# A macaron layer with two mixture-of-experts FFNs: where the first FFN's expert results are put, how empty rows are filled, who takes the roots

## The chip, the cores and the metric

One core of one Trainium2 chip runs the whole kernel in one launch. The metric is the device time in microseconds; a kernel is timed in several runs, and one more execution is profiled.

## The reference, cut to what matters

The input is x of 4 x 512 tokens with 256 features. Three residual steps follow each other, all in fp32:

```python
x = x + 0.5 * ffn(layernorm(x))      # FFN 0
x = x + attention(layernorm(x))      # 16 heads of 128, 4 sequences of 512
x = x + 0.5 * ffn(layernorm(x))      # FFN 1, the same weights
# ffn(t):
logits = t @ router_w.T              # 16 experts
w, e = top_k(softmax(logits), 2);  w = w / sum(w)
shared = silu(t @ sg) * (t @ su) @ sd                       # 256 hidden
routed = sum over k of w[k] * (silu(t @ gate[e[k]]) * (t @ up[e[k]])) @ down[e[k]]   # 128 hidden
return shared + routed
```

Each of the 2048 tokens goes to two experts, so an FFN has 4096 expert rows, and how many an expert gets is known only on the chip. Weights of attention come as codes and block scales that the kernel multiplies.

## The kernel before, in words

Matrix products are made of three products of a high and a low part (fp32r), `product`, lines 1324 to 1330. x lies in SBUF (`X`) as 16 tiles of 128 tokens; a quarter `q` or batch `b` is four of them (512 tokens).

**Routing.** For each quarter `statistics` (L857) takes mean and variance; `rstd` takes the root of 1/variance: ScalarE makes Ln and Exp (L608 to L615), VectorE one Newton step (L869). ScalarE and VectorE normalize into `rows`, TensorE transposes, `logits` (L1344) and `choose` pick the two experts, `ranks` and `positions` give each expert row its place in `xs_dram`, a DRAM array with a region of 2176 rows for each expert. GpSimd's `scatter` (L468) writes every tile of normalized rows twice, once for each choice, by indirect DMAs of 128 rows (L492); a row carries as word 257 the place of its result, which a small copy (L463, "marking") sets, so the second choice's marking waits for the first choice's landing.

**Empty rows.** Expert rows are worked through in 48 tiles of 128 rows, in 24 pairs; an expert's last tile has rows that nobody wrote. So VectorE's `free_rows` gives SP the row behind each expert's last one, and SP's `fills` (L321) copy 128 empty rows behind each expert, 16 DMAs (all before the first tile load in FFN 0, 12 in FFN 1). `tables_expert` and `tables` (L944, L956) make, on one partition, the list of tile offsets (`toff`) and of the tiles' experts (`words`), which SP and TensorE load into registers.

**Tiles.** `tiles` of PE, ACT and DVE (L1401, L647, L999) are one loop, shifted by stage: pair p+1 is transposed (L1418), pair p goes through gate and up, its silu and product follow, p-1 is transposed again (L1440), p-2 goes through down. ScalarE evicts a pair's result (L674) into one of two buffers `dnb`; GpSimd's `results` (L499) scatters each tile of it by an indirect DMA (L502) to `y_dram`, in the order of the tokens, at the places in word 257. The eviction waits until the buffer's scatters before have landed; SP's `tile_loads` (L332) wait for the landing too, as a tile's rows hold the places. In FFN 0 the expert weights' halves are split inside the loop, one chunk per pair (`split_hi`, `split_lo`, three staging buffers), 11 of 18 chunks before it (`PRE_CHUNKS`).

**Around the tiles.** The shared FFN runs in steps of 512 tokens: `EARLY` = 2 of its four steps before the tiles, the rest after (`shared_late`). When the results have landed, SP loads them for each batch (`y_loads`), VectorE adds them with their weights (`combine_half`), and the next normalization follows. GpSimd prepares attention's weight parts (`weights`, L522) that SP loads (`part`, L364; one codes DMA and four scales DMAs each); the first four parts are loaded behind the last tile load.

**Attention.** 64 units, one for a head and a batch. Tables written by hand name the unit in which an extra piece runs: `START` and `MID` (V blocks "V", transposes "Ta" and "T1"), `COMBINE`, `STATS` and `RSTD` (L277 to L292). In VectorE's order the insertion `before_scores` (L1178) stands ahead of the row maxima of the next unit; ScalarE's `exp_` waits for those. Between the units GpSimd also splits expert weights for FFN 1 and writes them to DRAM; SP loads them back near the end.

Of the kernel before, what the change touches and what calls it, by code (L numbers as in the profile page):

```python
# [5 lines left out]
P = 128  # L6
# [14 lines left out]
KT = D // P  # L21
# [6 lines left out]
LN_EPS = 1e-5  # L28
SM_SCALE = float(HD) ** -0.5
# [6 lines left out]
ROW = D + 1  # L36
NR = 48
# [9 lines left out]
PRE_CHUNKS = 11  # L47

EARLY = (2, 2)
FIRST_PRE = 3  # L50
SECOND_PRE = 9

FILLS_FIRST = (NE, 12)
# [4 lines left out]
C_ID, C_IOTA, C_J, C_EB, C_LT, C_I = 0, 128, 144, 160, 176, 432  # L58
C_POW = C_I + NR
C_N = C_POW + 6  # L60
# [47 lines left out]
class Views:  # L108
# [4 lines left out]
    "cst_in rw_in rw tri pads b_in bo_in bo bias w_hi w_lo e_in dv av pool_steps "  # L113
    "pre_in pre_mul pre_out "
# [11 lines left out]
def build(nc, t):  # L126
    with ExitStack() as ctx:
        def sb(name, shape, dt=F32):
# [15 lines left out]
        m.ln = sb("ln", [P, 2, 5, QB])  # L144
# [10 lines left out]
        m.tab = sb("tab", [1, 6, NE])  # L155
        m.frow = sb("frow", [1, NE], I32)
# [3 lines left out]
        m.mx = sb("mx", [P, QB])  # L160
        m.sm = sb("sm", [P, QB])
        m.ri = sb("ri", [P, QB])
        m.bank = [ctx.enter_context(nc.psum_tensor(f"bank{i}", [P, 512], F32)) for i in range(8)]
        m.xs_dram = [nc.dram_tensor(f"xs_dram{f}", (XROWS, ROW), F32, kind="Internal").ap() for f in range(2)]
# [22 lines left out]
        m.rows = Yw.rearrange("p (t d) -> p t d", t=NT)  # L187
        m.yb = Yw[:, 0:TOPK * QB * D].rearrange("p (b k t d) -> p b k t d", b=1, k=TOPK, t=QB)
        m.y1 = m.PT.rearrange("p l b n -> p (l b n)")[:, 0:TOPK * QB * D].bitcast(F32)\
            .rearrange("p (k t d) -> p k t d", k=TOPK, t=QB)  # L190
# [9 lines left out]
        m.ind = c.cut(NR // 2 * NE)[0:1].rearrange("p (t e) -> p t e", e=NE)  # L200
        m.te = c.cut(2 * NR)[0:1].rearrange("p (a t) -> p a t", a=2)
        m.rwT = c.cut(KT * NE).rearrange("p (k e) -> p k e", k=KT)
        m.sg = Pw[:, 4 * D:4 * D + 2 * S].rearrange("p (j n) -> p j n", j=2)
        m.dnb = Pw[:, 0:2 * 2 * D].rearrange("p (b n) -> p b n", b=2)
        m.sgr = Pw[:, 4 * D:4 * D + 4 * P].rearrange("p (b j n) -> p b j n", b=2, j=2)
# [39 lines left out]

        @block.tensor
        def _(pe):
            pe_program(nc, pe, m, s)


XS_F = 16 * (NR // NT)
RES_F = 16 * (NR // 4)


def chunk_place(m, c):

    if c < SH_CHUNKS:
# [1522 lines left out]
```

## Time and profile before

| | us |
|---|---|
| median of 3 runs (lowest, highest) | 1249.88 (1244.11, 1250.19) |
| the profiled execution's own time | 1238.46 |
| its span, first to last instruction | 1236.7 |
| TensorE busy | 1108.0 (90%) |
| VectorE busy | 856.8 (69%) |
| ScalarE busy | 719.2 (58%) |
| GpSimd busy | 372.7 (30%) |
| mean granted TensorE clock | 0.963 |

The span falls into routing and one half of the shared FFN (to 84 us), the first tile loop (to 174), a handover (to 212), attention (to about 1070), routing again (to 1115), the second tile loop (to about 1204) and an end. Busy shares are averages over these stages. The ends of matmuls are modelled, and a wait is put down to what came last by the profile.

### The profile page before, as it was taken

To read this page: it belongs to the slowest core of one execution; us is meant where nothing else is said; L and a number is where in the kernel's file an instruction comes from. 1 tells how busy PE (TensorE), PEld (TensorE's weight loads), DVE (VectorE), ACT (ScalarE), POOL (GpSimd) and SP (SyncE) were. 2 spreads that over 40 slices of the span, in tenths; PEclk is the share of its full clock that TensorE was granted. 3 is DMA by queue.
4 is the path that set the end of the run, shared out by engine and by line. 5 is a ranking of instruction groups with operands and counts; after the bars stand their busy time and mean duration, and the time that the engine had idled before them with its cause. 6 is when DMAs were issued, how large, how long until landed. Compare 5 with 4: busy or idle time off the path is not lost.

```text
span 1236.7 us, 20720 instructions
## 1 busy us (share of the span) xinstructions
PE 1108.0 (90%) x6360; PEld 957.0 (77%) x6360; DVE 856.8 (69%) x1837; ACT 719.2 (58%) x1485; POOL 372.7 (30%) x458
## 2 busy tenths in 40 slices
PE   5759984799999999999999999999999999858994
PEld 5648873687888878888888888888888877747884
DVE  7455436788777787877778777787777777653336
ACT  5226432666766766767767676676767666424441
POOL 2714567220003463400154320124001042342550
PEclk9869997899999999999999999999999999978997
DMA  4546435020013104400022430011000012655425
GB/s 172 186 151 185 139 102 165 10 69 1 1 54 118 41 24 153 129 5 1 18 65 87 144 95 1 9 35 53 1 1 1 2 62 105 236 171 144 135 81 204
DMA packets 58602, 103.76 MB, mean 84 GB/s; under 512 B 12756, under 2 KB 41819, under 8 KB 57952
## 3 DMA queue, kind: packets, MB, share of 16 engines
q1 hardware_dynamic: 50816, 85.60, 22.2%
q0 software_dynamic: 7680, 16.84, 3.8%
q8 instruction: 55, 0.90, 0.3%
q14 instruction: 51, 0.42, 0.1%
HBM read 70.89 MB, written 40.16 MB: 90 GB/s over the span
## 4 chain that ended last, share of the span: by engine, by line
PE 75%; DVE 7%; issue 6%; ACT 4%; DMA 3%; SPq 2%; another core or an unknown queue 2%; POOL 1%; POOLq 0%; DVEq 0%; ACTq 0%
PE bank L1327 14%; PE bank L1329 14%; PE bank L1328 14%; PE bank L1546 9%; PE bank L1554 5%; PE bank L1556 4%; PE bank L1555 4%; PE bank L1573 2%; PE bank L1572 2%; PE bank L1571 2%; PE bank L1418 1%; DMA y_dram<-work 1%; PE bank L1338 1%; POOL y_dram L502 1%
## 5 line engine op out<-in xcount | busy, mean ns | idle before, releaser
L1327 PE MATMUL bank<-R 128*128 128x512 f32 (+2 forms) x1056 | 405.0, 384 | 57.9 <-DVE X L996 21.3
L1328 PE MATMUL bank<-R 128*128 128x512 f32 (+2 forms) x1056 | 382.1, 362 | 0.0
L1329 PE MATMUL bank<-R 128*128 128x512 f32 (+2 forms) x1056 | 381.4, 361 | 0.0
L1327 PEld LDWEIGHTS bank<-R 128*128 128x128 f32 x1056 | 207.1, 196 | 99.0 <-issue 46.7
L1329 PEld LDWEIGHTS bank<-R 128*128 128x128 f32 x1056 | 206.7, 196 | 28.8
L1328 PEld LDWEIGHTS bank<-R 128*128 128x128 f32 x1056 | 207.7, 197 | 22.3
L1142 DVE TENSOR_REDUCE mx<-bank 128x1 f32<-128x512 f32 x256 | 174.5, 691 | 61.0 <-PE bank L1329 59.3
L736 ACT ACTIVATE work<-bank,mx 128x512 f32<-128x512 f32 x256 | 175.4, 690 | 59.2 <-DVE mx L1142 58.4
L1135 DVE SCALAR_TENSOR_TENSOR R<-bank,bias,R 128x512 fp32r<-128x512 f32 x192 | 143.7, 748 | 71.9 <-ACT R L730 70.5
L747 ACT ACTIVATE R<-bank 128x512 fp32r<-128x512 f32 x256 | 139.2, 598 | 65.9 <-PE bank L1546 65.7
L1155 DVE TENSOR_TENSOR R<-bank,R 128x512 fp32r<-128x512 f32 x256 | 167.6, 679 | 1.8 <-ACT R L747 1.0
L1546 PE MATMUL bank<-cst,work 128*128 128x128 f32 x1024 | 134.2, 274 | 13.3 <-issue 7.5
L730 ACT ACTIVATE R<-bank,bias 128x512 fp32r<-128x512 f32 x128 | 88.3, 690 | 90.0 <-PE bank L1329 90.0
L1546 PEld LDWEIGHTS bank<-cst,work 128*128 128x128 f32 x1024 | 116.5, 141 | 26.6 <-issue 13.7
L502 POOL DMA_INDIRECT y_dram<-work x96 | 94.9, 988 | 124.4 <-ACT work L674 102.1
L540 POOL CAST R<-work 128x256 fp32r<-128x256 f32 x64 | 26.2, 410 | 262.6 <-PE bank L1329 142.1
L1554 PE MATMUL bank<-R 128*128 128x512 f32 x256 | 100.3, 392 | 0.0
L1556 PE MATMUL bank<-R 128*128 128x512 f32 x256 | 99.8, 390 | 0.0
L1555 PE MATMUL bank<-R 128*128 128x512 f32 x256 | 99.6, 389 | 0.0
L741 ACT ACTIVATE work<-work,ri 128x512 f32<-128x512 f32 x128 | 87.2, 719 | 0.8 <-DVE ri L1147 0.8
L492 POOL DMA_INDIRECT xs_dram<-work,pos x64 | 64.6, 1010 | 45.7 <-DVE pos L934 26.7
L1151 DVE TENSOR_SCALAR work<-work,ri 128x512 f32<-128x512 f32 x128 | 71.0, 555 | 4.5
(125 smaller groups left out, 1549.7 us busy)
## 6 DMA issues: line engine op xcount, KB each, us to landing
work<-in_ffn_w SPq DMA_DIRECT2D x34, 384.0 KB, 4.6
work<-xs_dram SPq DMA_DIRECT2D x96, 128.5 KB
w_dram<-work SPq DMA_DIRECT2D x16, 768.0 KB, 4.0
R<-w_dram SPq DMA_DIRECT2D x16, 768.0 KB
work<-in_codes SPq DMA_DIRECT2D x64, 128.0 KB
work<-in_scales SPq DMA_DIRECT2D x256, 32.0 KB
R<-y_dram SPq DMA_DIRECT2D x10, 512.0 KB, 7.2
xs_dram<-in_empty SPq DMA_DIRECT2D x34, 128.5 KB, 3.1
```

Of the source, the lines that this page charges most:

```text
L736: nc.scalar.activation(m.Pm[:, qb, :], bank[2 + qb % 2][:], ACT.Exp, bias=m.mx[:, qb:qb + 1], scale=1.0, accum_out=m.sm[:, qb:qb + 1]).the ...
L747: nc.scalar.activation(m.PT[:, 0, kb, :], bank[4 + kb % 2][:], ACT.Copy).then_inc(s["t_hi"], 1)
L1135: v_.scalar_tensor_tensor(out=dst[:, 1, :], in0=bank[bk][:], scalar=m.bias[:, which, h:h + 1], in1=dst[:, 0, :].bitcast(F32), op0=ALU.add, ...
L1142: v_.reduce_max(m.mx[:, qb:qb + 1], bank[2 + qb % 2][:], AX_X, negate=True).then_inc(s["max"], 1)
L1155: v_.tensor_tensor(m.PT[:, 1, kb, :], bank[4 + kb % 2][:], m.PT[:, 0, kb, :].bitcast(F32), ALU.subtract)\
L1327: nc.tensor.matmul(out, ah, bh, start=(i == 0 and first), stop=False)
L1328: nc.tensor.matmul(out, ah, bl, start=False, stop=False)
L1329: last = nc.tensor.matmul(out, al, bh, start=False, stop=(i == n - 1))
L1546: ins = nc.tensor.transpose(bank[4 + kb % 2][:, qb * P:(qb + 1) * P], m.Pm[:, qb, kb * P:(kb + 1) * P], ident)
L1554: nc.tensor.matmul(bank[1][:], vh, ph, start=(kb == 0), stop=False)
L1555: nc.tensor.matmul(bank[1][:], vh, pl, start=False, stop=False)
L1556: ins = nc.tensor.matmul(bank[1][:], vl, ph, start=False, stop=(kb == QB - 1))
```

## The change

- FFN 0's results are stored by SP in the order of the tiles (`store`, one plain DMA for a pair, to `y_tiles`). After the tiles GpSimd gathers them for each token (`gather`, eight indirect DMAs for a batch), at places that VectorE works out inside the tile loop (`in_tiles`). Rows of FFN 0 carry no 257th word, so there is no marking. FFN 1 keeps the scatters of results; its rows of quarters 2 and 3 are marked in a second copy, so that they need not wait for landings. Result buffers are three.
- The 16 fills of FFN 0 become one indirect DMA of GpSimd, 16 rows of 256 words per partition. FFN 1's regions are filled whole (17 DMAs of SP, between attention's weight parts).
- The tables are made with one tile per partition and turned into a row by two small matmuls (`tables_row`).
- `rstd` is made by VectorE alone, from a bit trick's seed and three Newton steps; it stands right behind the statistics.
- Other first slots: `EARLY` = (1, 2), `PRE_CHUNKS` = 9 with nine chunks in the loop (`WITH_PAIR`, `CHUNK_AT`), batch 1's combine in unit 0, its statistics in unit 1, its transposes in unit 2, the V blocks and the other batches moved accordingly. ScalarE's normalizations of a batch stand in the unit of its statistics. `logits` goes over the two halves of the features outside. GpSimd's first four weight parts are multiplied (`scaled`) before the gather.

The diff, cut to its core:

```diff
-PRE_CHUNKS = 11
-EARLY = (2, 2)
+PRE_CHUNKS = 9
+WITH_PAIR = (2, 2, 1, 1, 1, 1, 1)
+CHUNK_AT = {2: 9, 3: 10, 4: 11, 6: 12, 8: 13, 10: 14, 12: 15, 14: 16, 15: 17}
+RESULTS = 3
+EARLY = (1, 2)
+STORE_AT = 11
...
-COMBINE = {0: (2, 0), 1: (2, 1), 3: (3, 0), 5: (3, 1)}
-STATS = {2: ("a", 2), 6: ("a", 3), 53: ("1", 0), 57: ("1", 1)}
+COMBINE = {0: ((1, 0), (1, 1)), 3: ((2, 0),), 4: ((2, 1),), 7: ((3, 0),), 8: ((3, 1),)}
+STATS = {1: ("a", 1), 5: ("a", 2), 9: ("a", 3), 53: ("1", 0), 57: ("1", 1)}
...
+    def store(p):
+        sp.wait_ge(s["r_ev"], p + 1)
+        sp.dma_start(m.y_tiles[2 * p * P:(2 * p + 2) * P, :].rearrange("(j p) d -> p j d", p=P),
+                     m.dnb[:, p % RESULTS].rearrange("p (j d) -> p j d", j=2)).then_inc(m.put[p % RESULTS], 16)
...   # in tile_loads, FFN 0
+                if f == 0 and i % 2 and i // 2 >= STORE_AT:
+                    store(i // 2 - STORE_AT)
+        if f == 0:
+            for p in range(NPAIR - STORE_AT, NPAIR):
+                store(p)
...   # sync_program
-    tile_loads(0, f0)
-    for n in range(4):
-        part(n)
-    results_landed(0)
-    y_loads(0, 0)
-    y_loads(0, 1)
+    tile_loads(0)
+    for n in range(PARTS_G):
+        part(n)
...   # between the parts of groups 1 to 3
+            e = (n - PARTS_G - HG) // 2
+            if n % 2 and e <= NE:
+                empty_region(e)
...   # pool_program, at quarter 3 of the scatters
+            pool.wait_ge(s["behind"], 1)
...
+            nc.gpsimd.indirect_dma_start(
+                out=m.xs_words, out_offset=bass.IndirectOffsetOnAxis(ap=m.fill[:, 0:1], axis=0),
+                in_=m.X.rearrange("p t d -> p (t d)"), in_offset=None).then_inc(s["fill0"], 16)
...
+    def gather(b):
+        wait(pool, s["comb0"], b)
+        for k in range(TOPK):
+            for i in range(QB):
+                n = QB * b + i
+                nc.gpsimd.indirect_dma_start(
+                    out=m.yb[:, 0, k, i, :], out_offset=None, in_=m.y_tiles,
+                    in_offset=bass.IndirectOffsetOnAxis(ap=m.gpos[:, k, n:n + 1], axis=0))\
+                    .then_inc((m.y_first, m.y_in)[k][b], 16)
...
+    for kind, hh in values:
+        scaled(0, kind, hh)
+    pool.wait_ge(s["r_dn"], NPAIR)
+    for kind, hh in values[:3]:
+        halved(0, kind, hh)
+    for sem in m.put:
+        pool.wait_ge(sem, 16 * (NPAIR // RESULTS))
+    pool.wait_ge(s["gpos"], TOPK)
+    gather(0)
+    halved(0, *values[3])
+    weights(0, others[:5])
+    gather(1)
...   # dve_program, rstd
+        st.link(v_.tensor_scalar(ve, m.mv[:, tiles, 1], LN_EPS, None, ALU.add))
+        st.link(v_.tensor_scalar(a.bitcast(I32), ve.bitcast(I32), 1, None, ALU.logical_shift_right))
+        st.link(v_.tensor_scalar(r0.bitcast(I32), a.bitcast(I32), -1.0, ROOT_SEED, ALU.mult, ALU.add))
+        for new in (r0, r0, m.rstd[:, 0, tiles]):
+            st.link(v_.scalar_tensor_tensor(out=a, in0=ve, scalar=-0.5, in1=r0, op0=ALU.mult, op1=ALU.mult))
+            st.link(v_.tensor_tensor(b, a, r0, ALU.mult))
+            st.link(v_.scalar_tensor_tensor(out=new, in0=b, scalar=1.5, in1=r0, op0=ALU.add, op1=ALU.mult))
...   # end of attention, VectorE
+    positions(1, 2, K0)
     y_add(UNITS // 4 - 1)
...
-    shared_h(1, 0)
     choose(1, 3, L0)
     positions(1, 3, K0)
-    free_rows(1, CNT)
+    counted(1, CNT)
+    tables(1)
+    shared_h(1, 0)
+    tables_row(1)
     shared_h(1, 1)
```

## Rows read from the trace of the kernel before

**Rows 1.** The page, chain that ended last: shares of the span by engine

```profile
PE 75%; DVE 7%; issue 6%; ACT 4%; DMA 3%; SPq 2%; another core or an unknown queue 2%; POOL 1%; POOLq 0%; DVEq 0%; ACTq 0%
```

**Rows 2.** Timeline of TensorE (start, length): the same step of two units

```profile
538.68 1.04 PE L1546 MATMUL bank<-cst,work 128*128 128x128 f32 x8
...
551.41 1.04 PE L1546 MATMUL bank<-cst,work 128*128 128x128 f32 x8
```

**Rows 3.** Busy time by stretch: length, engines, granted clock, DMA share, GB/s

```profile
75.00:100.00 25.00, 16.76 (x105) 15.92 (x103) 11.89 (x20) 10.20 (x20) 1.98 (x2) 0.71 0.60 182
```

**Rows 4.** Timeline of GpSimd in the first tile loop [idle before, releaser]

```profile
151.20 0.98 POOL L502 DMA_INDIRECT y_dram<-work  x1 [2.28 <-ACT work L674]
152.48 0.98 POOL L502 DMA_INDIRECT y_dram<-work  x1 [0.30 <-issue]
...
158.29 0.98 POOL L502 DMA_INDIRECT y_dram<-work  x1 [2.26 <-ACT work L674]
```

**Rows 5.** Timeline of TensorE: transposes of two pairs early in the loop

```profile
96.57 0.60 PE L1418 MATMUL bank<-cst,work 128*128 128x128 f32 x4
...
99.38 0.60 PE L1418 MATMUL bank<-cst,work 128*128 128x128 f32 x4
```

**Rows 6.** Timeline of GpSimd: first and last of 32 row scatters

```profile
19.97 1.14 POOL L492 DMA_INDIRECT xs_dram<-work,pos  x1 [11.00 <-DVE pos L934]
...
66.71 0.96 POOL L492 DMA_INDIRECT xs_dram<-work,pos  x1 [0.30 <-issue]
```

**Rows 7.** Timeline of SP's DMA issues ahead of the tiles

```profile
52.67 15.79 SPq L329 DMA_DIRECT2D xs_dram<-in_empty  x16
...
77.76 0.89 SPq L351 DMA_DIRECT2D work<-xs_dram  x2
```

**Rows 8.** Timeline of TensorE: loop's first transposes, last down product, attention's first projection

```profile
83.96 1.96 PE L1418 MATMUL bank<-cst,work 128*128 128x128 f32 x8 [7.04 <-issue]
...
173.40 0.28 PE L1329 MATMUL bank<-R 128*128 x1
...
211.68 0.47 PE L1327 MATMUL bank<-R 128*128 128x512 f32 x1 [4.01 <-DVE R L891]
```

**Rows 9.** Timeline of VectorE: one small instruction of the root

```profile
12.14 0.16 DVE L877 TENSOR_TENSOR ln<-ln 128x4 f32<-128x4 f32 x1
```

**Rows 10.** Busy time by stretch: the fullest DMA stretch of the handover

```profile
184.00:188.00 4.00, 3.83 (x22) 2.99 (x20) 0.82 (x1) 0.77 (x2) 3.74 (x6) 1.00 1.01 401
```

**Rows 11.** Timeline of SP: the first V weight part's scales

```profile
156.05 1.83 SPq L369 DMA_DIRECT2D work<-in_scales  x4
```

**Rows 12.** Timelines: SP's issue of part 5's scales, GpSimd waiting for scales

```profile
187.09 1.82 SPq L369 DMA_DIRECT2D work<-in_scales  x4
192.01 0.85 POOL L529 TENSOR_SCALAR work<-work 128x256 f32<-128x256 f32 x1 [2.77 <-DMA work<-in_scales]
```

**Rows 13.** Timeline of TensorE, unit 0

```profile
235.06 1.97 PE L1546 MATMUL bank<-cst,work 128*128 128x128 f32 x8 [4.77 <-DVE R L1155]
```

**Rows 14.** Timelines: VectorE's row maxima in a unit, ScalarE's normalizations of a batch

```profile
545.49 1.37 DVE L1142 TENSOR_REDUCE mx<-bank 128x1 f32<-128x512 f32 x2 [1.53 <-PE bank L1329]
...
230.97 2.07 ACT L621 ACTIVATE work<-X,rstd 128x256 f32<-128x256 f32 x4 [0.82 <-DVE rstd L879]
```

**Rows 15.** Busy time by stretch: 200 us of attention

```profile
400.00:600.00 200.00, 197.73 (x1081) 169.53 (x1080) 154.57 (x287) 136.77 (x279) 59.91 (x68) 1.00 0.19 57
```

**Rows 16.** Timeline of TensorE: second shared step, tiles of FFN 1

```profile
1107.24 0.58 PE L1327 MATMUL bank<-R 128*128 128x256 f32 x1 [4.45 <-DVE R L989]
...
1115.47 1.09 PE L1418 MATMUL bank<-cst,work 128*128 128x128 f32 x4 [3.83 <-issue]
1117.59 1.46 PE L1418 MATMUL bank<-cst,work 128*128 128x128 f32 x4 [1.02 <-DMA work<-xs_dram]
...
1192.42 0.60 PE L1418 MATMUL bank<-cst,work 128*128 128x128 f32 x4
```

**Rows 17.** Timeline of GpSimd: the last result scatter

```profile
1207.44 1.12 POOL L502 DMA_INDIRECT y_dram<-work  x1 [0.30 <-issue]
```

More of the change, by code:

```diff
@@ L36 @@
 ROW = D + 1
+FILL = P * NE // P
 NR = 48
@@ new lines, in tile_loads @@
+    def tile_loads(f):
+        sp.wait_ge(s[f"toff{f}"], 1)
+        if f == 0:
+            sp.wait_ge(s["pads"], 16)
+            sp.wait_ge(s["fill0"], 16)
+            sp.wait_ge(s["scat0"], 16 * TOPK * NT)
+        else:
+            for name in ("scat_a", "scat_b"):
+                sp.wait_ge(s[name], 16 * 2 * QB)
+            sp.wait_ge(s["scat_2"], 16 * NT)
+        width = ROW if f else D
+        i0 = 0
+        for group in GROUPS:
+            _, at = nc.values_load_multi_w_load_instructions(
+                m.toff[0:1, i0:i0 + group], engines=[SP_ENGINE], min_val=0, max_val=XROWS - P)
+            i0 += group
+            for i, v in enumerate(at, i0 - group):
+                if f == 0 and i in CHUNK_AT:
+                    chunk(CHUNK_AT[i])
@@ L439, in sync_program @@
     expert(11)
-    f1 = fills(1)
-    for _ in range(FILLS_FIRST[1] + 1):
-        next(f1, None)
-    tile_loads(1, f1)
-    results_landed(1)
+    tile_loads(1)
+    for sem in m.res:
+        sp.wait_ge(sem, RES_F)
     for b in range(B):
-        y_loads(1, b)
+        y_loads(b)
     for b in range(B):
@@ new lines, in halved @@
+    def halved(g, kind, hh):
+        codes = m.raw[:, 0, part_of(g, kind, hh) % 4, :]
+        if kind == "v":
+            wait(pool, s["v"], 16 * g - 16)
+            hi, lo = (m.Wv[:, g % 2, l, :, hh * HD:(hh + 1) * HD] for l in range(2))
+            src = codes.rearrange("p (k n) -> p k n", k=KT)
+        else:
+            hi, lo = (m.Wh[:, hh, "qko".index(kind), l, :] for l in range(2))
+            src = codes
+            if g > 0:
+                pool.wait_ge(s["y" if kind == "o" else kind], 16 * g - 3 + hh)
+        st.link(nc.gpsimd.tensor_copy(hi, src))
+        nc.gpsimd.tensor_tensor(lo, src, hi.bitcast(F32), ALU.subtract).then_inc(s["wprep"], 1)
@@ L1119, in dve_program @@
     normalize("a", 0, xna(0), (0, 1))
-    for step in range(EARLY[0], QB):
-        shared_add(0, step)
-    combine_half(1, 0)
+    shared_h(0, 7)
     xt_los("a", 0, 2)
-    combine_half(1, 1)
+    shared_add(0, 3)
     def v_lo(n, bk=0):
@@ L1181, in before_scores @@
             y_add(u // 4 - 1)
-        if u in COMBINE:
-            combine_half(*COMBINE[u])
+        for half in COMBINE.get(u, ()):
+            combine_half(*half)
         if u in STATS:
@@ L1708, in pe_program @@
     pe.wait_ge(s["e_in"], 16 * NE)
-    tiles(1)
-    shared_late(1)
+    tiles(1, word)
+    gate_up(1, 2 * EARLY[1])
+    gate_up(1, 2 * EARLY[1] + 1)
+    pe.wait_ge(s["r_ev"], 2 * NPAIR)
+    for step in range(EARLY[1], QB):
+        if step + 1 < QB:
+            gate_up(1, 2 * step + 2)
+        down(1, step)
+        if step + 1 < QB:
+            gate_up(1, 2 * step + 3)
 def _constants(np):
```

563 lines of the change are left out of this document (269 added, 294 removed), and 6 rows, old and new, of the table SEMAPHORES.

## The prediction

> **What bounds the kernel now.** I read the page's chain of waits first. TensorE carries 75% of it, the same few matmul lines over and over [rows 1]; an attention unit (64 of them) takes 12.73 us where nothing else is inserted, TensorE being busy all of it [rows 2]. What is to be had lies at the two FFNs, so I went to the table of busy time by stretch next: ahead of the first FFN's expert tiles TensorE is busy 67% and the granted clock is 0.71 [rows 3], that is, most of the time at 1.2 GHz; the stretch ahead of the second FFN's looks the same. Third, GpSimd's timeline inside the tile loop: four result scatters of 0.98 us, 1.29 us from start to start, then 2.3 us of waiting for ScalarE's eviction, and the pattern comes back after 7.1 us [rows 4]. A result buffer (two of them) is free only when its scatter has landed, so two pairs of tiles cost 7.1 us, 3.55 a pair. Where the buffers don't bind, at the start of the same loop, a pair takes 2.81 us [rows 5], which is TensorE's work. So the tile loops are bound by the results' way out, the stretch before them by a serial chain.
>
> **Ahead of the first tiles.** GpSimd's 32 row scatters run from 19.97 to 67.67 us [rows 6], 1.27 us each plus eight marking copies and their waits for landings. SP then does 16 fills (52.67 to 68.46), two more weight chunks and only at 77.76 the first tile load [rows 7]; TensorE starts at 83.96 [rows 8]. The change drops the markings (the first FFN's rows no longer carry a target), the 16 fills (SP gets free) and two chunks, and adds one indirect fill. GpSimd: 20.2 + 33 x 1.28 + 1.5 for slow ones = 64; landed 66; register load and first tile load 67; first transposes 71, by half the issue-to-start time of before, since the chunks no longer stand in front. VectorE and TensorE are ready sooner: count at 45.5, the tables now one tile per partition, about 12 instructions, 3.5 us, instead of 24 x 16 elements on one partition; one shared step, done at 64. The root by VectorE adds 8 small instructions per group of tokens, 0.16 us and a gap of 0.04 each [rows 9], 1.6 us; GpSimd's queue of scatters hides it (its next rows are ready 2 us or more before it gets to them). Term: -13.0 us. The fill's price is open: it writes 16 KB per partition, 2.1 MB, and no row has such an indirect DMA. From below: another 0.96 us scatter, its data at 401 GB/s [rows 10] gone in 5 us while eight scatters follow. From above: as if each of its 2048 rows of 1 KB cost what a scatter's row does, 16 x 0.96 = 15.4 us on GpSimd, and the first tiles 14 us later. I take the lower end, since the count of descriptors per partition is one. The Trainium skill's "DMA: Bandwidth & Descriptors", Anatomy of one DMA, calls descriptor generation small and variable, which stands with the lower end; no run here shows it.
>
> **First tile loop.** Results leave by one plain store of SP per pair, and tile loads no longer wait for results. Before: 83.96 to 173.68 = 89.7 us [rows 8]. After: 12.6 us to the fifth pair's transposes as before (half clock), 19 x 2.83, 8.1 for the last pairs' way through, 2 for late chunks (nine now ride in the loop, two per pair at first, on three staging buffers) = 76.5. Term: -13.2. SP has 2 loads, a store and a chunk per pair, 4 x 0.45 us, so it doesn't bind. End of the last down product: 147.5.
>
> **From there to attention's first projection: what gets worse.** Before, the four V weight parts were issued from 156.05 on (the first one's scales, 1.83 us) [rows 11], under the loop, and lay ready. Now they stand on SP behind the last store, which waits for the last eviction: 148.3, then 4 x 2.33 us of issue (four scales loads as in rows 11, and 0.5 for a codes load), 157.6; a part landed 3.7 us after its last issue when GpSimd waited for it (issued till 188.91, used at 192.01) [rows 12], so 161.3. GpSimd multiplies all four parts before its gather: last at 162, then three parts split, 1.2 us each, 165.7; eight gathers at 1.29, 176; landed 179. VectorE combines the second half till 181.3, statistics 1.9, root 2.5, normalize 1.1 (186.8), transposes 2 and the last shared down product 4 at a rising clock: first projection at 193.3, that is 45.8 us behind the loop against 38.0 before (173.68 to 211.68 [rows 8]). Term: +7.8. Gain at this point: 18.4.
>
> **Attention.** Unit 0 had a stall of 4.77 us for the next batch's normalization, with 2 us at half clock after it [rows 13]; both go, since the transposes move to unit 2: -6.8. But statistics, root and (for units 1, 5, 9) ScalarE's four normalizations, 2.07 us [rows 14], now sit in one unit ahead of the row maxima. VectorE has 1.53 us to spare there [rows 14]; statistics 1.9 and root 2.5 are 4.4, and ScalarE's exp waits for the normalizations behind them: 4.2 us later than normal, 0.4 of it slack, 3.8 lost in each of three units, 11.4, less about 1.3 that two of them cost now, -2.6. Unit 0 takes two combine halves (3.4 us, 1.8 over the slack); the other insertions cost 1.2. Term: +5. Units 53, 57 and 60 have the root too, 4.4 - 1.5 - the 0.7 that they lose now: about +2 each, +6. 17 region fills of 2.2 MB between the weight parts: hidden, GpSimd being busy 60 of 200 us there [rows 15]; +1, up to 10 if parts come late. Together +12.
>
> **Second FFN.** The 16 fills (12 ahead of the first load) go, and scatters follow one another (a second copy of the rows), so rows are there at about 1100. But tiles also wait for two shared steps, and these get no earlier: their first VectorE product moves behind the tables. Down product 0 starts at 1097.5 instead of 1092.4, product 1, which now starts at 1107.24 after a 4.45 us wait for VectorE [rows 16], at 1112; start of tiles 1118 against 1115.47 for the first pair and 1117.59 for the second [rows 16]: +0.5. In the loop three result buffers remove the landing from the cycle: GpSimd needs 2.57 a pair, TensorE 2.83, so 20 pairs go from 3.40 ((1192.42 - 1117.59) / 22 [rows 16]) to 2.83, -11.4; the last scatter ends about 1197 instead of 1208.6 [rows 17] and what follows it is unchanged. Term, all of it: -11.6.
>
> **Sum**, against the profiled execution of 1238.46 us (span 1236.7): -13.0 - 13.2 + 7.8 + 12 - 11.6 = -18.0, 1220.5. The median of the three timed runs is 11.4 above that execution; from it the same sum gives 1231.9, and that is my number. I call 0.5% (6.2 us) what the measurement can tell from no change.
>
> **Rivals.** (a) As forecast, gain 10 to 27: 0.50. (b) What I charge attention and the handoff is mostly hidden: VectorE's later stretches absorb the root and parts land sooner: +20 becomes +6, total -32, 1218. For: VectorE is idle 23% of attention [rows 15]. Against: exp stands behind the normalizations in program order. 0.24. (c) The fill is dear, 15.4 us: -18 + 13 = -5, 1245; against it, the fill is one descriptor per partition. 0.09. (d) The other side: the loops don't follow the buffers but the round trip ScalarE, VectorE, TensorE inside a pair, and stay at 3.5 us: the gain of both loops but 1, 25, is lost, +7, 1257. It decides where pairs take more than about 3.25 us. For it: TensorE waits 0.7 to 1.1 us for VectorE's product in every second pair; against it, 2.81 at the start of both loops. 0.09. The last 0.08: less gain than forecast by several small things.
>
> (a) and (b) are faster, and a little of (c); (c) mostly and half of the rest same; (d) and a little slower: 0.79, 0.11, 0.10. Range 1210 to 1251; it leaves out the far end of (b) and most of (d).
>
> **What would show it.** Right: first tile transposes near 71; pairs at 2.8 us in both loops with no wait of ScalarE for landings; GpSimd's first gather near 166, waiting for scales loads before it; first projection near 193; units 1, 5, 9 at 15 us; a last scatter that ends 12 us earlier relative to the loop's start. Wrong: a fill above 3 us on GpSimd, pairs above 3.2 us, a gather before 160, or units with a root at 13 us.

## The result, and the profile after

The changed kernel takes 1284.53 us (median of 4 runs) against 1247.59 us of the kernel before (4 runs): ratio 1.0322, 95% interval 1.028 to 1.0364. It is slower by 3.2% where 1.4% faster was forecast. Its profiled execution took 1282.39 us with a span of 1280.6, the one before 1238.46 and 1236.7: 43.9 us more where the sum said 18.0 less.

In the page's chain of waits TensorE's share falls from 75% [rows 1] to 69%, while the time for which the profile shows no cause ("issue") goes from 6% to 9%, VectorE's from 7% to 9% and GpSimd's from 1% to 3%:

```profile
PE 69%; DVE 9%; issue 9%; SPq 3%; ACT 3%; DMA 3%; POOL 3%; another core or an unknown queue 1%; POOLq 0%; DVEq 0%; ACTq 0%
```

Splitting both executions at the same steps of TensorE (first and last tile transposes of a loop, first transposes of units 0, 13, 53 and 63) and at the end of the last result scatter says where. The three columns on the right are of runs told below (the kernel before and the changed one again, and a mended version), made in groups of runs in which the kernel before took 1203 us and not 1245 to 1248.

| stage, us | before | after | difference | before, e16 | after, e18 | mended, e17 |
|---|---|---|---|---|---|---|
| to the first tile transposes | 83.96 | 76.46 | -7.5 | 79.2 | 74.4 | 70.0 |
| first tile loop, first to last transposes | 78.0 | 83.8 | +5.8 | 69.7 | 84.7 | 78.8 |
| to unit 0 | 65.8 | 69.3 | +3.4 | 62.9 | 68.6 | 59.7 |
| units 0 to 12 | 180.0 | 211.3 | +31.3 | 180.0 | 207.9 | 181.2 |
| units 13 to 52 | 514.3 | 514.7 | +0.3 | 514.3 | 514.5 | 514.7 |
| units 53 to 62 | 138.7 | 145.0 | +6.3 | 136.8 | 142.0 | 136.7 |
| to the second loop's first transposes | 54.6 | 52.7 | -1.9 | 50.2 | 52.8 | 50.2 |
| to the end of the last scatter | 93.1 | 95.4 | +2.3 | 81.2 | 95.3 | 77.4 |
| to the end | 28.1 | 32.0 | +3.9 | 28.4 | 27.4 | 28.3 |

**First loop.** TensorE's timeline at its start (start, length, group, [idle before, what ended it]):

```profile
76.46 1.09 PE L1491 MATMUL bank<-cst,work 128*128 128x128 f32 x4 [2.70 <-DMA work<-xs_dram]
82.96 1.12 PE L1491 MATMUL bank<-cst,work 128*128 128x128 f32 x4 [5.41 <-DMA work<-xs_dram]
92.63 0.77 PE L1491 MATMUL bank<-cst,work 128*128 128x128 f32 x4 [4.06 <-DMA work<-xs_dram]
...
117.14 0.58 PE L1390 MATMUL bank<-R 128*128 x1 [6.95 <-DVE R L959]
```

The first line answers to the first of [rows 8]. The other three are stalls inside the loop, and SP's own timeline has their cause: its load of a weight chunk (in_ffn_w) waits from 80.6 to 88.66 with the tile loads of the next pair behind it, and the first result store leaves only at 110.67, behind the load of the pair 11 ahead:

```profile
79.71 0.85 SPq L391 DMA_DIRECT2D work<-xs_dram  x2
88.66 0.34 SPq L339 DMA_DIRECT2D work<-in_ffn_w  x1
89.18 0.85 SPq L391 DMA_DIRECT2D work<-xs_dram  x2
...
110.67 0.43 SPq L365 DMA_DIRECT2D y_tiles<-work  x1
```

What the chunk loads wait for is VectorE's split (L959), which frees the staging buffer. SP's waits between 60 and 135 us (us in total, times, longest):

```profile
SPq L339 <- DVE R L959: 24.7, 4, 13.1
```

For the landing of that first result store ScalarE's eviction waits, and with it all behind it:

```profile
113.71 0.60 ACT L754 ACTIVATE work<-bank 128x512 f32<-128x512 f32 x1 [6.68 <-DMA y_tiles<-work]
```

From then on a pair takes 2.80 us, 14 times in a row. So the last down product's end comes at 168.1 instead of 173.7.

**The fill** that was in doubt cost GpSimd one instruction of 1.22 us, after 1.77 us of idle time:

```profile
59.07 1.22 POOL L566 DMA_INDIRECT xs_dram<-X,fill  x1 [1.77 <-issue]
```

**Units with a root.** Unit 1 took 21.4 us, not 12.7. VectorE's timeline, with ScalarE's and TensorE's line behind it: statistics 252.09 to 253.90, root 253.93 to 258.00, ScalarE's four normalizations from 258.04, only then the exp (L811) for which TensorE waits 4.09 us:

```profile
252.09 1.39 DVE L921 BATCH_NORM_STATS2 stats<-X 128x6 f32<-128x256 f32 x4
253.93 0.29 DVE L931 TENSOR_SCALAR ln<-mv 128x4 f32<-128x4 f32 x1
...
257.84 0.16 DVE L938 SCALAR_TENSOR_TENSOR rstd<-mv,rstd 128x4 f32<-128x4 f32 x1
```

```profile
258.04 2.07 ACT L692 ACTIVATE work<-X,rstd 128x256 f32<-128x256 f32 x4 [5.67 <-DVE rstd L938]
```

```profile
260.83 0.79 PE L1390 MATMUL bank<-R 128*128 128x512 f32 x1 [4.09 <-ACT work L811]
```

The product behind that wait takes 0.79 us where the same one took 0.50 and 0.48 earlier in the unit: the granted clock has dropped to its lower level, 1.2 GHz, for a part of the unit. The busy time by stretch (columns as in [rows 3]) has a mean granted clock of 0.87 over the first 12.7 of unit 1's 21.4 us and 1.00 over 200 us later:

```profile
244.70:257.40 12.70, 9.44 (x47) 7.26 (x45) 8.06 (x23) 3.55 (x6) 10.79 (x16) 0.87 0.18 52
440.00:640.00 200.00, 197.65 (x1086) 169.93 (x1085) 153.40 (x283) 135.94 (x276) 60.81 (x69) 1.00 0.51 174
```

The second line, against [rows 15], shows also that the region fills slow no unit: nine of the 17, of 2.2 MB each, are issued in it (DMA share 0.51, before 0.19), and TensorE is busy 197.65 of the 200 us, before 197.73.

**Second loop.** TensorE's waits in it, by cause (columns as above): six are for tile loads, where the kernel before had one of 1.02 us [rows 16].

```profile
PE bank L1491 <- DMA work<-xs_dram: 13.0, 6, 2.9
PE bank L1390 <- DVE R L1076: 1.2, 1, 1.2
```

### The profile page after: what moved, and what is told of

Its sections match the earlier page's. It is cut to its first block, busy times and chain, and to the rows that moved or that the text cites. A ratio compares the mean times of both kernels' runs of the same rounds, so it can differ in the third digit from the quotient of the medians.

```text
span 1280.6 us, 20561 instructions
## 1 busy us (share of the span) xinstructions
PE 1119.0 (87%) x6368; PEld 968.0 (76%) x6368; DVE 873.5 (68%) x1930; ACT 718.6 (56%) x1463; POOL 354.6 (28%) x427
## 4 chain that ended last, share of the span: by engine, by line
PE 69%; DVE 9%; issue 9%; SPq 3%; ACT 3%; DMA 3%; POOL 3%; another core or an unknown queue 1%; POOLq 0%; DVEq 0%; ACTq 0%
PE bank L1390 14%; PE bank L1392 13%; PE bank L1391 13%; PE bank L1621 8%; PE bank L1629 4%; PE bank L1630 4%; PE bank L1631 4%; PE bank L1646 2%; PE bank L1648 2%; PE bank L1647 2%; POOL xs_dram L502 2%; DMA work<-xs_dram 1%; SPq L391 1%; SPq L381 1%; PE bank L1401 1%
## 5 line engine op out<-in xcount | busy, mean ns | idle before, releaser
L1390 PEld LDWEIGHTS bank<-R 128*128 128x128 f32 x1056 | 209.5, 198 | 93.4 <-ACT work L811 27.0
L1392 PEld LDWEIGHTS bank<-R 128*128 128x128 f32 x1056 | 208.7, 198 | 29.5
L1391 PEld LDWEIGHTS bank<-R 128*128 128x128 f32 x1056 | 210.2, 199 | 22.7
L811 ACT ACTIVATE work<-bank,soft 128x512 f32<-128x512 f32 x256 | 175.3, 688 | 77.1 <-DVE soft L1214 77.0
L1214 DVE TENSOR_REDUCE soft<-bank 128x1 f32<-128x512 f32 x256 | 174.4, 691 | 63.9 <-PE bank L1392 62.3
L1621 PE MATMUL bank<-cst,work 128*128 128x128 f32 x1024 | 134.9, 275 | 10.9 <-issue 8.3
L805 ACT ACTIVATE R<-bank,bias 128x512 fp32r<-128x512 f32 x128 | 88.3, 690 | 94.7 <-PE bank L1392 89.5
L1621 PEld LDWEIGHTS bank<-cst,work 128*128 128x128 f32 x1024 | 116.6, 141 | 25.0 <-issue 15.6
L1629 PE MATMUL bank<-R 128*128 128x512 f32 x256 | 102.3, 400 | 0.0
L1630 PE MATMUL bank<-R 128*128 128x512 f32 x256 | 101.5, 397 | 0.0
L1631 PE MATMUL bank<-R 128*128 128x512 f32 x256 | 101.3, 396 | 0.0
L587 POOL TENSOR_TENSOR work<-work 128x256 f32<-128x256 f32 x64 | 49.5, 774 | 141.4 <-DMA work<-in_scales 140.0
L816 ACT ACTIVATE work<-work,soft 128x512 f32<-128x512 f32 x128 | 87.0, 718 | 0.8 <-DVE soft L1219 0.8
L1223 DVE TENSOR_SCALAR work<-work,soft 128x512 f32<-128x512 f32 x128 | 73.6, 575 | 4.5
## 6 DMA issues: line engine op xcount, KB each, us to landing
xs_dram<-in_empty SPq DMA_DIRECT2D x16, 2184.5 KB, 11.8
```

The costliest lines, as they stand in the source:

```text
L811: nc.scalar.activation(m.Pm[:, qb, :], bank[2 + qb % 2][:], ACT.Exp, bias=m.mx[:, qb:qb + 1], scale=1.0, accum_out=m.sm[:, qb:qb + 1]).the ...
L1214: v_.reduce_max(m.mx[:, qb:qb + 1], bank[2 + qb % 2][:], AX_X, negate=True).then_inc(s["max"], 1)
L1390: nc.tensor.matmul(out, ah, bh, start=(i == 0 and first), stop=False)
L1391: nc.tensor.matmul(out, ah, bl, start=False, stop=False)
L1392: last = nc.tensor.matmul(out, al, bh, start=False, stop=(i == n - 1))
L1621: ins = nc.tensor.transpose(bank[4 + kb % 2][:, qb * P:(qb + 1) * P], m.Pm[:, qb, kb * P:(kb + 1) * P], ident)
```

## The experiments

The runs were made in five groups, each with the kernel before in it. A run's median stands beside that of the kernel before in its group, with the ratio and its 95% interval. The kernel before itself differed: 1245, 1201, 1247, 1203 and 1203 us in the five groups, 1248 in the first measurement. So differences are taken within a group or between groups of the same kind, or stage by stage. The expectations speak of chips that differ. That is not shown: on record the first group (1245) and the fifth (1203) have the same chip number, 0; the others have 13, 4 and 8.

**e1, the loads' wait in the second loop.** A row buffer (16 of them) also holds the target that its tile's result scatter reads. The changed kernel waits on a ring of 6 semaphores with the index of the new tile; as 16 is no multiple of 6, that is for the tile 12 back in every third pair.

```diff
-sp.wait_ge(m.res[i % (2 * RESULTS)], 16 * ((i - NT) // (2 * RESULTS) + 1))
+sp.wait_ge(m.res[(i - NT) % (2 * RESULTS)], 16 * ((i - NT) // (2 * RESULTS) + 1))
```

> The changed kernel; in the second FFN a tile load waits for the scatter of the tile whose row buffer it takes (16 tiles back) instead of, for every third pair, the one 12 tiles back. Theory A (the load's wait is what stalls TensorE, six times, 13.0 us in all, in the second tile loop): the six stalls go, pairs take 2.8 to 2.9 us throughout, about 10 us less than the changed kernel, some 1274. Rival B (the loads are late because GpSimd's scatters are, and the wait only shows it): the stalls move, less than 3 us is gained, 1281 to 1285.

1273.5 (before 1245.3, ratio 1.0219, 1.0191 to 1.0248, the changed kernel's 1.0322): about 11 us less. That is theory A's time, but not by its way alone. The six waits for loads, 13.0 us, are gone, and the loop is only 7.1 us shorter (88.3 for 95.4; 4.1 more come behind it): a pair takes 3.24 us on average, not 2.8, as other waits have come in, which is half of rival B:

```profile
PE bank L1390 <- DVE R L1076: 4.5, 5, 1.3
PE bank L1513 <- DVE work L1083: 1.7, 3, 0.8
```

**e2, two result buffers** (`RESULTS = 2`, else as changed; four semaphores divide 16, so the wait is right by itself).

> The changed kernel with two result buffers instead of three (then the load's wait is for the tile 16 back as well). Theory A (buffers set the pair's period, as I had it before the change): 3.4 to 3.5 us a pair in the second loop as in the kernel before, so slower than with three buffers and the right wait by 10 us, about even with the changed kernel. In the first loop the eviction waits for a plain store instead of a scatter: 2.8 to 3.2 us a pair. Rival B (period set by the round trip between the engines): no difference to three buffers, about 2.8 in both loops.

1276.3 (1.0254, 1.0222 to 1.0286). Pairs in the second loop take 3.28 us against e1's 3.24, in the first 2.80 as with three, once it runs; only the stall for the first store grows, from 11.5 us between two pairs to 13.0. The number of buffers sets neither period: rival B in that; but its 2.8 for both loops is wrong as well. GpSimd still issues four scatters and then waits for ScalarE, as in [rows 4]:

```profile
1193.39 0.99 POOL L540 DMA_INDIRECT y_dram<-work  x1 [2.52 <-ACT work L754]
...
1197.27 0.98 POOL L540 DMA_INDIRECT y_dram<-work  x1 [0.30 <-issue]
1200.22 0.98 POOL L540 DMA_INDIRECT y_dram<-work  x1 [1.97 <-ACT work L754]
```

**e3, the attention's early units as before.** V products, transposes and combine halves go back to nearly the units that they had, batch 1 is normalized ahead of unit 0's transposes, the root comes one unit after the statistics.

```diff
-COMBINE = {0: ((1, 0), (1, 1)), 3: ((2, 0),), 4: ((2, 1),), 7: ((3, 0),), 8: ((3, 1),)}
-STATS = {1: ("a", 1), 5: ("a", 2), 9: ("a", 3), 53: ("1", 0), 57: ("1", 1)}
+COMBINE = {1: ((2, 0),), 2: ((2, 1),), 4: ((3, 0),), 5: ((3, 1),)}
+STATS = {2: ("a", 2), 6: ("a", 3), 53: ("1", 0), 57: ("1", 1)}
+RSTD = {u + 1: x for u, x in list(STATS.items()) + list(STATS_END.items())}
```

> The changed kernel with the attention's early units arranged as in the kernel before: one V product per unit, batch 1 combined and normalized ahead of unit 0 and transposed in it, statistics in units 2 and 6, root (still by VectorE) one unit later. Theory A (the arrangement of units 1 to 12 costs the 33 us): unit 1 to 13 takes 162 to 166 us instead of 196, unit 0 some 8 longer, 1284 becomes about 1258. Rival B (gathers, GpSimd's weight work or the DMAs of these 200 us slow the units): they stay at 15 to 18 us wherever the work stands, less than 10 gained.

1265.4 (1.0155, 1.0127 to 1.0183), 19 us less than the changed kernel's 1284.5. Units 1 to 12 take 171.1 us (after 196.1, before 161.9), unit 0 26.0: most of theory A's 162 to 166, with 11 of the 25 us spent again in unit 0, where TensorE waits 10.67 us:

```profile
244.77 1.97 PE L1636 MATMUL bank<-cst,work 128*128 128x128 f32 x8 [10.67 <-DVE R L1231]
```

Ahead of it VectorE combines batch 1 and makes its statistics and root, and ScalarE normalizes, till 242.8, one after the other. VectorE began at once when its earlier work was done; the gathers had been issued by 219.6. So it is the place of this chain in the order that costs:

```profile
230.51 5.63 DVE L1106 SCALAR_TENSOR_TENSOR X<-work,wt,X 128x256 f32<-128x256 f32 x8
240.69 2.07 ACT L692 ACTIVATE work<-X,rstd 128x256 f32<-128x256 f32 x4 [10.98 <-DVE rstd L942]
```

**e4, only the pairs of V products, in the kernel before.**

```diff
-START = {1: ("V", 4), 2: ("V", 5), 3: ("V", 6), 4: ("V", 7), 6: ("V", 8), 7: ("V", 9), 8: ("V", 11),
+START = {3: ("V", 4), 4: ("V", 6), 5: ("Ta", 2, 0), 6: ("Ta", 2, 1), 7: ("V", 8), 8: ("V", 10),
...
+MID = {3: ("V", 5), 4: ("V", 7), 7: ("V", 9), 8: ("V", 11), 11: ("V", 13), 12: ("V", 15),
```

> The kernel before with only the order of the V products and transposes changed: two V products in units 3, 4, 7, 8, 11 and 12 as in the changed kernel, none in the others, the transposes of batches 2 and 3 at the start of units 5, 6, 9, 10. Theory A1 (pairs of V products are most of the loss): each such unit 2.7 us over 12.73, the others 1.4 less or no less, +10 to +16 us. Theory A2 (the serial chain statistics, root, normalization, exp in one unit is most of it): pairs cost at most what the empty units give back, 0 to +5 us.

1245.1 (1.0021, 0.9984 to 1.0059); units 0 to 12 take 183.6 us for 180.0. A unit with two takes 14.6 to 15.6, those without give back most. Theory A2.

**e5 and e6, the root on VectorE, and then in the statistics' own unit,** both in the kernel before (13 dependent instructions in the place of five and of ScalarE's logarithm and exponential; in e6 `rstd(ph, q)` moves behind `statistics(ph, q)`, and ScalarE's four normalizations of a batch move with it into that unit).

> The kernel before with only the root changed: all of it on VectorE (13 small instructions instead of 4 and two of ScalarE's), in the same places, one unit after the statistics. Theory C (the root itself is cheap, its place is not): within 3 us of the kernel before, the units with a root at most 2 us longer. Rival D (13 dependent instructions cost their 2.6 us wherever they stand): 1.5 to 2 us for each of 5 units, and 2 ahead of the first tiles, +8 to +12 us.

> As the run with the root on VectorE, but the root in the same unit as its statistics and ScalarE's four normalizations behind it in that unit, as in the changed kernel. Theory C: units 2 and 6 now take 17 to 19 us (statistics, root, normalization, exp one after another), units 53 and 57 as the changed kernel's 16.9 and 16.7; about +15 us against the kernel before. Rival D: nothing more than in that run.

e5: 1217.6 (before 1201.4, ratio 1.0127, 1.0099 to 1.0155). e6: 1229.3 (1.0231, 1.0202 to 1.026), 11.8 more; units 2 and 6 take 19.2 and 18.2 us (e5: 12.8 and 12.9), 53 and 57 15.3 (12.9 and 12.9). Neither theory holds whole: the root costs 16 us here before its place counts, more than C's 3 and D's 8 to 12, and its place 12 more, which is C's half. In e6 the chain of unit 2 is the one of the changed kernel; TensorE's line in it:

```profile
262.73 0.80 PE L1316 MATMUL bank<-R 128*128 128x512 f32 x1 [4.52 <-ACT work L728]
```

**e14 and e16, the same root and the kernel before, with traces of one group.**

> The kernel before with the root on VectorE, one unit after the statistics, again, now with a trace of the kernel before from the same chip. Theory M (the root costs little apart from its place): 3 to 5 us in all by the stages, ratio 1.003. Rival N (the 1.27% measured on the other chip is its price everywhere): ratio 1.01 or more, and some stage other than the units must show it.

> The kernel before itself, for its trace on this chip: attention's units as in the first profile within 3 us of 833; pairs in the second loop at 3.35 us as on the first chip or 2.8 as on the second.

e14: 1216.2, e16: 1204.4 (before 1203.4; e14's ratio 1.0107, 1.0081 to 1.0132; e16's 1.0007). The spans differ by 12.2 us, in many places: first tiles 4.4 later, to unit 0 2.9, units 0 to 12 2.8, 53 to 62 1.5, between attention and the second loop 1.9, less 1.3 at the end. Rival N.

**e7 and e11, the first loop's start.** e7: stores behind the load of the pair 6 ahead, chunks later. e11: also 11 chunks ahead of the tiles, their splits in ScalarE's and VectorE's idle time.

```diff
-STORE_AT = 11
+STORE_AT = 6
-PRE_CHUNKS = 9
-WITH_PAIR = (2, 2, 1, 1, 1, 1, 1)
+PRE_CHUNKS = 11
+WITH_PAIR = (1, 1, 1, 1, 1, 1, 1)
```

> The changed kernel; in the first tile loop a result is stored behind the load of the pair 6 ahead, not 11 ahead, and the nine late weight chunks are loaded and split later (1, 1, 1, 1, 2, 2, 1 by pair). Theory E (SP's order makes both stalls: the loads behind the chunks, 12.9 us of waiting, and ScalarE's eviction that waits for the first store, 6.9 us): the 11.5 us gap is gone, transposes come at 2.8 us from the fifth pair on, the loop is 10 to 15 us shorter, 1284 becomes about 1272. Rival F (the DMAs' bandwidth is the limit there, not the order): the loads land as late as before, less than 5 us gained.

> The changed kernel with its first loop's start mended: 11 weight chunks ahead of the tiles, whose splits now fill idle time of ScalarE and VectorE there, one chunk per pair behind them, and the store of a result behind the load of the pair 6 ahead. Theory E (SP's order and the chunks behind which the tile loads stand make all the stalls at the start of the loop): 2.8 to 3.4 us a pair from the second on, first to last transposes 68 us instead of 83.8, 14 us gained. Rival F (DMA bandwidth): the 2.1 MB of chunks and tiles land as late as before, under 7 us gained, as the half mend did (77.7 us).

e7: 1264.1 in a group with before at 1201.4; its loop takes 77.7 us, e8's in the same group, with the changed kernel's start, 83.4. These 5.7 us lie between E's 10 to 15 and F's 5, and tell little: three gaps of 5 to 6 us remain, where the late chunks now stand. e11: 1272.9, 13 less than the changed kernel in its group (1286.0); the loop takes 71.3 us against 83.8, though its first transposes come 2.3 us later (78.8). Theory E. What is left inside the loop is waiting for loads, 5.9 us in four waits, where the changed kernel had 10.2 for loads and 6.9 for the store.

**e8 and e15, half of the scatters.**

```diff
-        for i in range(NR):
+        for i in range(0, NR, 2):
```

(The rows of `y_dram` that are left out are written once, by two plain DMAs ahead.)

> The changed kernel with the exact wait, and in the second FFN only every other tile's results scattered (24 scatters instead of 48; the results of the other tiles are left out). Theory G (GpSimd's scatters, 2.6 us a pair, are what holds a pair at 3.4 us in the second loop, whatever the number of result buffers): pairs at 2.8 to 2.9 us, 10 to 13 us less than with all scatters, about 1261. Rival H (something else in the second loop, such as the order of ScalarE's work): pairs stay at 3.3 to 3.5.

> The changed kernel with the exact wait and only every other tile's results scattered in the second FFN (the others are left out), on a chip to be compared with the kernel before. If the kernel before has pairs of 3.4 us there: theory G (the scatters hold the pair) gives 2.8 us here, rival H 3.3 or more. If it has 2.8, the run says nothing new.

1252.0 and 1250.8 (ratios 1.0417 and 1.0393), pairs 2.80 us. But in these groups the kernel before too has 2.80 with all its scatters (e5 and e16), so they don't tell G from H. GpSimd's timeline in e16, the kernel before, second loop: for twelve pairs it waits about 0.5 us after every two scatters, that is, once a pair, and later there is a string of eight; in [rows 4] it waits 2.3 us after every four:

```profile
1120.65 0.98 POOL L502 DMA_INDIRECT y_dram<-work  x1 [0.59 <-ACT work L674]
1121.93 0.98 POOL L502 DMA_INDIRECT y_dram<-work  x1 [0.30 <-issue]
1123.39 0.98 POOL L502 DMA_INDIRECT y_dram<-work  x1 [0.48 <-ACT work L674]
1124.67 0.98 POOL L502 DMA_INDIRECT y_dram<-work  x1 [0.30 <-issue]
...
1141.25 0.98 POOL L502 DMA_INDIRECT y_dram<-work  x1 [1.57 <-ACT work L674]
```

**e9, e10 and e18, both kernels again.**

> The kernel before itself, profiled on the chip of this group. In the last group it took 1201 us on one chip where the first two groups had 1245 on another. Theory I (the chips differ in how the result scatters go: 2.8 us a pair in both tile loops there, 3.4 to 3.55 here): whichever chip this is, the attention's 833 us are the same within 3 and the two loops carry the difference. Rival J (a general difference, such as DMA speed or clock): it spreads over all stages.

> The changed kernel itself on the same chip. Theory I: where the kernel before has pairs of 2.8 us, nothing of the change's gain in the loops is to be had, and it is 60 to 80 us slower than the kernel before (ratio 1.05 to 1.065); where the kernel before has 3.5 us pairs, the ratio is 1.03 as first measured. Rival J: 1.03 on every chip.

> The changed kernel itself. If the kernel before takes 1246 here, 1.03; if it takes 1203, the loops' scatters cost the kernel before nothing there, and the changed kernel, whose stalls remain, is at 1.055 to 1.065.

e9: 1246.1 (before 1246.7); its profiled execution took 1254.3 us and is not used. e10: 1286.0, ratio 1.0349 (1.0271 to 1.0428). e18: 1269.2 where before took 1202.8, ratio 1.0543 (1.0508 to 1.0577). These are theory I's ratios, not J's; that a chip makes the difference is not shown. For the kernel before, attention is the same in both kinds of group within 2 us (the table), and 29.4 of the 34.0 us lie where rows or results are scattered: 4.7 ahead of the first tiles, 8.4 and 11.9 in the loops, 4.4 ahead of the second. Other traces say the same: e4's, of the 1245 group, has 78.6 and 93.2 in the loops, e5's and e14's, of groups at 1201 and 1203, have 72.0 and 69.6, 80.6 and 80.8. The changed kernel, whose first loop has no scatters, gains nothing there (84.7 for 83.8), and nothing in its second, which its wait for loads holds (95.3 for 95.4). TensorE's waits in the second loop of e16 are the other side of it:

```profile
PE bank L1418 <- DMA work<-xs_dram: 6.3, 4, 4.3
PE bank L1327 <- DVE R L1004: 0.6, 1, 0.6
```

In the first profile of the kernel before the same view has nine waits for VectorE's product (L1012) and for the low part of its transpose (L1018), 5.8 us in all, as e1 has (above); in e16 there is none of these:

```profile
PE bank L1440 <- DVE work L1012: 3.6, 5, 0.9
PE bank L1327 <- DVE R L1018: 2.2, 4, 0.8
```

**e12, e13 and e17, all mends.** e12: e1, e3 and e11 together, and the V weight parts loaded between the loop's tile loads. e13: batch 1's results gathered into a buffer of their own right behind batch 0's and combined ahead of the units, the units as in the kernel before, the store 8 pairs ahead. e17: ScalarE's root again, two result buffers, parts loaded between the last stores.

```diff
     gather(0)
-    halved(0, *values[3])
-    weights(0, others[:5])
     gather(1)
-    weights(0, others[5:])
+    halved(0, *values[3])
+    weights(0, others[:8])
     gather(2)
+    weights(0, others[8:])
```

> The changed kernel with the exact wait, the units as in the kernel before, the mended first loop, and the first V weight parts loaded under the loop, each between two tile loads, so that the gather starts on the last store's landing. Sum by what the single runs gave and by my reading: 10 + 19 + 14 + 7 (the gather 12 us earlier, of which combine and shared steps let 7 through) = 50 less than the changed kernel; about 1233 on a chip where the changed kernel takes 1284. Rival: the mends overlap (the units' stall of batch 1 grows when attention starts earlier), 35 or less.

> The version with all mends, and now batch 1's results gathered right behind batch 0's into a buffer of their own and combined ahead of unit 0, the later batches' work in the units where the kernel before has it, the V weight parts loaded two pairs later and the store behind the load of the pair 8 ahead. Theory K (the units' loss is the order of this work alone): units 0 to 12 take 180 to 184 us as in the kernel before instead of 195, the two gaps of 5 us in the first loop go: 15 to 18 us less than the version with all mends, about 1223 where the kernel before takes 1246. Rival L (gathers or the VectorE root cost in the units wherever they stand): unit 0 stays above 20 us, less than 8 us gained.

> The version of the run before last, with the root again by ScalarE's logarithm and exponential with one step on VectorE, two result buffers instead of three, and the V weight parts loaded between the last stores instead of between tile loads. Theory (root 12 us as measured alone, part loads 5 us at the loop's end, number of buffers without effect): 15 us less than that version: 1200 on a chip where the kernel before takes 1203 (ratio 0.995 to 1.0), 1222 to 1228 on one where it takes 1246 (0.98 to 0.985). Rival: the root's cost is hidden in this arrangement, 5 us less at most, ratio 1.007 or 0.99.

e12: 1240.6 (before 1246.7; 0.9975, 0.9939 to 1.0011), 45 less than the changed kernel in its group. Units 0 to 12 still take 194.9. GpSimd's timeline has its first gather at 166.88, in the changed kernel (second line) at 185.23:

```profile
166.88 1.04 POOL L555 DMA_INDIRECT work<-y_tiles,gpos  x1 [0.45 <-issue]
```

```profile
185.23 1.04 POOL L551 DMA_INDIRECT work<-y_tiles,gpos  x1 [0.45 <-issue]
```

e13: 1216.1 (before 1203.4; 1.0113, 1.0089 to 1.0136), units 0 to 12 185.5: 9 of the 15 us that e12's lost, mostly theory K; but unit 0 takes 22.3 us, as rival L has it. e17: 1198.9 (before 1202.8; 0.9969, 0.9957 to 0.9981), units 0 to 12 181.2 and unit 0 18.9; the first tiles 4.5 us earlier than e13's, the first loop 2.0 longer. Three things changed together here; by the stages it is the root that gives. TensorE's wait in unit 0 is down to what it was before, 4.77 us [rows 13]:

```profile
215.61 1.97 PE L1671 MATMUL bank<-cst,work 128*128 128x128 f32 x8 [4.74 <-DVE R L1268]
```

It is faster than both kernels, by 0.3% than the one before and by 5.5% than the changed one in the same group (1269.2). Its first loop still has one gap of 10 us between two pairs, in which ScalarE's eviction waits 5.92 us for a store's landing; how it does where the kernel before takes 1246 was not measured.

## Why the prediction was wrong, step by step

- *First tiles, -13.0*: measured -7.5. The fill was as cheap as I took it. The step that failed is "GpSimd's queue of scatters hides it", the root. It does not: the first scatter starts at 22.08 instead of 19.97 [rows 6], GpSimd waits 1.46 and 2.42 us for positions of later groups, and the last scatter ends at 70.4, not 64. e14 prices the root at 4.4 us here. e17, with ScalarE's root, has the first scatter at 20.05, no such wait, and the last one's end at 64.
- *First tile loop, -13.2*: measured +1.9 (91.6 us from the first transposes to the end of the last down product, 89.7 before). The steady pair was right, 2.80. What failed is "SP has 2 loads, a store and a chunk per pair, so it doesn't bind": its load by time was right, but each chunk waits for a split, each store for an eviction, and the tile loads stand behind them. TensorE waits 17.1 us inside the loop; e11 made the loop 12.5 us shorter.
- *Handover, +7.8*: 7.7 (168.1 to 213.8 against 38.0 us before). Right in sum; the gather started at 185.2, not 166, as the loop ended late, and counted from the loop's end 1 us sooner than I had it, with 1 us more behind it. There the root took 4.57 us, not 2.5. That GpSimd waits for the scales' loads first was right (172.96, idle since the loop's start). One row was misread without harm: [rows 12] give 3.1 us from a part's last issue to its use, not 3.7.
- *Attention, +12*: 37.5 from the first projection to unit 63. This is the largest error, and all but 6 us lie in units 0 to 12. I charged units 1, 5 and 9 3.8 us each; unit 1 took 8.7 over 12.7, unit 5 5.8 and unit 9 2.4. The root takes 4.07 us in unit 1 and 2.55 in unit 5, where GpSimd is idle (VectorE's instruction of 0.16 us took 0.58 and 0.65 beside GpSimd's work), and a stall is followed by products at half clock. Nor did I charge the combine halves of units 4 and 8, where y_add and two V products meet them (18.4 and 18.5 us). The order as a whole is what cost: e3 gives back 14 of the 31 us; e13 and e17, of groups in which the changed kernel has 207.9 us, give back 22 and 27 of 28. The V pairs alone cost 3.6, and how the rest divides over the single pieces of work was not measured. The region fills were right. So was the sum of units 53 to 62 (+6.3), by luck: I had 2 us in each of three units, and units 53 and 57 took 4.0 and 3.7 more, unit 60 nothing.
- *Second FFN, -11.6*: +4.3. Two things. "In the loop three result buffers remove the landing from the cycle": they removed nothing, e1 and e2 have 3.24 and 3.28 us a pair. I had read a buffer's wait out of [rows 4], where GpSimd waits for an eviction; that the eviction itself waited for a landing no row said, and the trace of the kernel before says no. Of ScalarE's waits in its first loop, those ahead of the eviction (L674) come to 3.2 us in all, one of them for a landing, while the silu waits for TensorE 21.6 us in nine waits and 13.5 more that the profile does not name:

```profile
ACT work L660 <- PE bank L1329: 21.6, 9, 3.8
ACT work L674 <- DMA y_dram<-work: 1.2, 1, 1.2
```

  And I took the loads' wait for right in its index; with the right one the kernel is 11 us faster (e1). The prologue part came 1.9 us earlier, not 0.5 later; and my own terms, +0.5 and -11.4, make -10.9, not -11.6. Why the last stretch took 3.9 us more is not settled: it took 32 us in e3, e8, e10, e11 and e15 as well, and 27.4 to 28.4 in e1, e2, e7 and e18.

One more row was misread, though no term hangs on it: [rows 3] are of 75 to 100 us, of which 16 lie in the tile loop. Ahead of the tiles (0 to 84 us) TensorE is busy 56% of the time and the mean granted clock is 0.89, not 0.71.

Rival (d), slower because the loops stay at 3.5 us, had the sign and 1257 us for 1284.5. Its mechanism, waits going round between the engines of a pair, fits the second loop in the groups where the kernel before takes 1246 (the waits for VectorE above), and not the first. The stalls of SP's order and the units stood in no rival.

What holds a pair at 3.2 to 3.6 us with scatters in some groups of runs and at 2.8 in others stays open. It is neither the number of buffers (e2) nor the pace of GpSimd's issue, 1.29 us from one scatter's start to the next in both kinds. In the groups at 1245 to 1248 a loop without scatters, the changed kernel's first, has 2.80 too; that speaks for theory G, but no run there leaves scatters out. The traces narrow it. In e16, with all scatters, ScalarE's silu starts 0.04 us after the recorded end of the gate and up products that it waits for, in 44 of 48 pairs:

```profile
1118.46 0.28 PE L1329 MATMUL bank<-R 128*128 x1
1118.79 0.38 ACT L660 ACTIVATE work<-bank 128x256 f32<-128x256 f32 x1 [0.78 <-PE bank L1329]
```

In the first trace of the kernel before it does so for the first four or five pairs of a loop, and for nearly all later ones it starts 0.4 to 2.9 us after that end, with ScalarE idle for it in every second pair:

```profile
1152.46 0.28 PE L1329 MATMUL bank<-R 128*128 x1
1155.42 0.38 ACT L660 ACTIVATE work<-bank 128x256 f32<-128x256 f32 x1 [3.67 <-remote]
```

In the changed kernel's first loop, in the same kind of group but without scatters, it is 0.04 us again in 22 of 24 pairs. The ends of matmuls are modelled, so the trace can't tell products that ended later than recorded from a signal that came late.

## What to carry to other kernels

A queue that has time to spare still delays everything behind an instruction of it that waits: for each instruction put into it, find what it waits for and what stands behind. Before a buffer is added, find the row in which the writer waits for the reader's landing; a reader that waits for the writer is no sign of it. A small dependent chain (here 13 instructions of 0.2 us) is not small in a unit in which another engine's work and then TensorE stand behind it; the same instructions, and ScalarE's normalizations behind them, cost 12 us less in four places when they stood one unit later (e5 against e6).

## What the runs showed of the hardware

- One indirect DMA that writes 16 KB from each of 128 partitions occupied GpSimd for 1.22 us in the first trace of the changed kernel and 0.96 us in e18's; one that writes 1 KB takes 0.96. The Trainium skill's "DMA: Bandwidth & Descriptors", Anatomy of one DMA, has descriptor generation as small and variable; these times agree with it.
- The same kernel (before) took 1201 to 1203 us in three groups of runs and 1245 to 1248 in three, at nearly the same mean granted clock (0.96 to 0.97). Most of the difference of two traces, 29 of 34 us, lies in the stages with scatters, and there ScalarE starts up to 2.9 us after the recorded end of TensorE's products that it waits for, against 0.04. Whoever compares two kernels from different groups can be off by more than this change.
- The root's 13 small VectorE instructions took 2.53 to 2.63 us in ten of twelve places of the changed kernel, three of them while GpSimd issued indirect DMAs; in the two places where GpSimd did elementwise work beside them, at 201 and 254 us, they took 4.57 and 4.07, some of them 0.57 to 0.67 us instead of 0.16.
